# Moving the last cell's value products eleven steps later, and the first output pair's sums and halves thirteen, in a conditional attention kernel

## The chip, the cores and the metric

The kernel runs on one core of one Trainium2 chip. The metric is the device time of one execution in microseconds, shown as the median of several runs.

## The reference

The input x is 32 sequences of 128 rows by 1024 columns in fp32. Two residual layers are applied:

```python
w = weights[conditions]                       # one 128x128 matrix for each sequence
x = x + einsum('bct,bcd->bdt', x, w)          # first layer
q, k, v = proj(x, Wq) * min(cond, 4), proj(x, Wk), proj(x, Wv)    # 16 heads of 64
scores = einsum('bhqd,bhkd->bhqk', q, k) / 8, causal mask, softmax
out = einsum('bhqk,bhkd->bhqd', attn, v)
x = x + einsum('bsd,ed->bse', out, Wo)        # second layer
```

All products are done in fp32 accuracy: each operand is split into a high and a low half (names ending in H and L), and a product is three matmuls (high by high, low by high, high by low; lines 710 to 712).

## The kernel before

The 32 sequences are taken in eight groups of four. Attention goes by **cells**: a cell is one group and two heads for each of q and k; there are 64 cells, n = 0 to 63, of 16 **steps** each. A step is three 128x512 matmuls on TensorE. Every other operation of every engine has a time in steps in a table (an `At`), and each engine's program walks the same times in order and issues what stands there. So the tables fix the order on each engine, and semaphores fix the rest; an instruction that waits holds everything behind it on its engine. The order is also that of the DMAs: SP and ACT both issue DMAs, and a DMA that stands behind a wait on its engine is issued only after it.

The part of the program that matters starts at `T_END`, the end of the last cell's projections. I write **step 20** for `T_END` + 20. The names used are these:

- **Scores and softmax of cell 63** at steps 5 to 12; the transposed probabilities are moved by ten small DMAs (line 1530, at step 15), split by ACT (`half_at`, line 1045, step 25) and POOL (`ptl_at`, line 1336, steps 25.75 and 27.25) into `t_PS`, and multiplied with the values by TensorE (`pv_at`, line 815). A cell has two such **value products**, P = 126 and 127 for the last one, into one PSUM tile `p_PV`. After each, ACT copies (`other_at`, lines 1052 and 1053), DVE sums (`own_at`, line 1229) and POOL adds (`at_at`, line 1339) the result, and SP stores it (line 1656). The second product waits for the DVE sums of the first (`dve_M`).
- **Plain output steps**: steps 0 to 63, eight blocks o = 0 to 7 of eight steps, each block into one of the three banks `p_PJ`. DVE adds a block to the rows of x that SP loaded (line 1266; call it **sum o**), and SP stores it (line 1680, **store o**). SP loads the rows for o = 4 to 7 (line 1511, **row load o**) into the tile of o - 4, after store o - 4 has landed.
- **Output pairs**: from `T_PAIR` = step 64 on, 14 pairs q of 28 steps. A pair needs only seven products of four steps each (i = 0 to 6, line 710 to 712 into `p_LP` and `p_SC`, or `p_PJ` for odd q) in place of eight. POOL forms four sums of the attention rows (`S_add`, lines 1359 to 1369), ACT and DVE split seven operands into halves (`A_high`, line 1080, and `A_low`, line 1239; **half 0 to 6**). The products take halves in the order 0, 4, 1, 5, 3, 2, 6. ACT copies product 0 (line 1088, `f_at`), DVE gathers the others (`c_at`, lines 1250 to 1261), POOL adds x (line 1377).
- **Loads around them**: SP loads the attention rows of pairs 0 and 1 (line 1586, `yp_load`, steps 24 and 24.25) and x of pairs 0 and 1 (line 1598, `xp_load`). ACT issues the last three quarter pairs of Wo from its own queue (line 965, `O_fetch`): 2 x 1 MB each at steps 26.5 (k = 6), 38.5 (k = 4) and 46 (k = 7). I call them **fetches 6, 4 and 7**. They have only a wait for TensorE's last projection, long past.

The waits that matter later are few: product 2 waits for ACT's copy of product 0, which for q = 0 waits until the store of P = 126 has landed, since they share a tile; product 3 waits for the first gather, for q = 0 also for the store of P = 127; POOL's first sum of pair 1 waits for half 6 of pair 0; x of pair 0 is loaded when store 7 has landed; product 6 waits for the fourth gather, which needs POOL's three additions of x.

```python
v = a + (27.25 + 3.25 * k if last else 29 + 4.5 * k)   # a is step 5 for the last cell
early = t - PAIR                                        # t is step 64 for q = 0
```

Of the kernel before, what the change touches and what calls it, by code (L numbers as in the profile page):

```python
# [17 lines left out]
PAIR = 28  # L18
# [27 lines left out]
def cond_attention(nc, x, idx, cond, w0, wq, wk, wv, wo, mask_d, ident_d, out):  # L46
# [14 lines left out]
    with ExitStack() as ctx:  # L61
# [182 lines left out]
        def block(kind, item):  # L244
            bank_of[kind, item] = len(order) % 3
            before[kind, item] = order[-3] if len(order) >= 3 else None
            order.append((kind, item))
# [62 lines left out]
        for p in range(2, NP):  # L310
            t = T_SEV + PAIR * (p - 2)
# [5 lines left out]
        for c in range(4):  # L317
            T_load.put((10, 13, 30, 39)[c], c)
            for i in range(4):
                t = (24, 33, 42, 51)[c] + i  # L320
# [3 lines left out]
        for p in range(2, NP):  # L324
            t = T_SEV + PAIR * (p - 2)
# [25 lines left out]
        for m in range(16):  # L351
            t = T_SEV + PAIR * (2 + m // 2) + (10.5, 23.25)[m % 2]
# [9 lines left out]
        for j in range(NGRP):  # L362
            t0 = T_ATT + STEPS * j
            for c in range(NC):
                n = 4 * j + c
                for i, kind in enumerate("qk"):
                    block(kind, n)
                    for d in range(DC):
                        step_at.put(t0 + 16 * c + 8 * i + d, (kind, n, d))
                done = t0 + 16 * c + 8  # L370
                late = 2.5 if n else 0
                q_ev.put(done + late, n)
                ql_ev.put(done + late + 1, n)
                done += 8
                kh_ev.put(done + 0.25, n)
                kl_ev.put(done + 1, n)
                a = done + 5
                for u in range(GB):
                    k = u // 2
                    sc_at.put(a + k, GB * n + u)  # L380
                    mask_at.put(a + 1 + 2 * k, GB * n + u)
                    exp_at.put(a + (2, 3, 4, 5)[u], GB * n + u)
                move_at.put(a + 10, n)
                for k in range(2):
                    P = 2 * n + k
                    recip_at.put(a + 4 + 2 * k, P)
                    norm_at.put(a + 4.25 + 2 * k, P)
                    turn_at.put(a + 7.5 + 1.5 * k, P)
                    last = n == 4 * NGRP - 1
                    half_at.put(a + (20 if last else 25.25) + 0.5 * k, P)  # L390
                    ptl_at.put(a + (20.75 if last else 26) + 1.5 * k, P)
                    v = a + (27.25 + 3.25 * k if last else 29 + 4.5 * k)
                    own = v + (1.75 if n >= 4 * NGRP - 2 else (1.75, 8.5)[k])
                    for z in range(2):
                        pv_at.put(v, 2 * P + z)
                    other_at.put(v + 0.75, P)
                    own_at.put(own, P)
                    at_at.put(own + 1.25, P)

            if j and j != NG:  # L400
                for i in range(8):
                    X_load.put(t0 - STEPS + ((25.5, 41.5)[i // 4] if j in (1, NG + 1) else (9.5, 25.5, 41.5)[i // 3]), (j, i))
            for k in range(2):
                V_load.put(t0 + ((-11, 2.75)[k] if j == 0 else -38.5 + 16 * k if j == NG else -6.5), (j, k))
            for u in range(GB):
                v_split.put(t0 + ((17, 19, 27.75, 28.75)[u] if j == 0 else 3.75 + u + 14 * (u // 2)), (j, u))
        t = T_ATT + STEPS * (NG - 1)
# [7 lines left out]
        for b in range(GB):  # L415
            t = T_END + (-70.5, -54.5, -38.5, -22.5)[b]
# [30 lines left out]
        yp_load, xp_load, S_add, A_high, A_low, R_at, f_at, c_at, x_at, o_store = (At() for _ in range(10))  # L447
        for q in range(NPAIR):
            t = T_PAIR + PAIR * q
            early = t - PAIR  # L450
            yp_load.put(T_END + (24, 24.25)[q] if q < 2 else t - PAIR - 8, q)
            xp_load.put(t + 5 if q == 0 else t - PAIR + 8, q)
            for i in range(4):
                S_add.put(early + (1, 3, 7, 12)[i], (q, i))
            for i in range(7):
                A_high.put(early + (1, 2, 3, 5.5, 6.5, 10, 15)[i], (q, i))
                A_low.put(early + (2, 3, 4, 6.5, 7.5, 11, 16.5)[i], (q, i))
                R_at.put(t + 4 * i, (q, i))
            f_at.put(t + 4.25, q)
            for i, d in enumerate((8, 12, 16, 20, 24, 28)):  # L460
                c_at.put(t + d + 0.25, (q, i))
                if i in (1, 3, 4, 5):
                    o_store.put(t + d + 1, (q, i))
            for i, d in enumerate((11, 13, 17.5) if q == 0 else (5, 10, 17.5)):
                x_at.put(t + d, (q, i))
# [1255 lines left out]
```

## Time and profile before

| what | before |
|---|---|
| median of 3 runs | 1570.99 us (1570.8 to 1571.9) |
| span of the profiled execution | 1569.4 us |
| runs less span | 1.6 us, taken as the execution's time around its span |
| TensorE busy | 1559.1 us (99%) |
| DMA traffic | 341 MB, mean 218 GB/s |

The profile is of one execution; times in it are from the start of its span. TensorE is busy nearly all the time, so the kernel's time is TensorE's work at its clock plus the few times in which it waits. "q1" is the DMA queue of SP, "q10" that of ACT; both use the same 16 DMA engines.

### The profile page before, as it was taken

Reading aid. Unit: us, or ns where it says so; the run is one execution under the profiler, and the core shown is the slowest. Engines: PE = TensorE matmul, PEld = TensorE weight load, DVE = VectorE, ACT = ScalarE, POOL = GpSimd, SP = SyncE. Lnnn points to the kernel's source line nnn. Section 1 sums busy time; section 2 is a strip of 40 time slices with the busy share of each in tenths; the row PEclk is TensorE's granted clock in tenths of the full one; section 3 lists DMA queues with packets and bytes.
Section 4 is the critical chain, followed back from the end, with each engine's and each line's share of the span. In section 5 each row is a group of like instructions: output and inputs, shape, how many; then the busy total and the mean of one; then the engine's idle time right before and its main releaser. Section 6 shows DMA issues by size and latency. Waiting matters only on the chain.

```text
span 1569.4 us, 23424 instructions
## 1 busy us (share of the span) xinstructions
PE 1559.1 (99%) x7563; PEld 1311.9 (84%) x7563; DVE 980.4 (62%) x1748; ACT 818.9 (52%) x2221; POOL 856.6 (55%) x752
## 2 busy tenths in 40 slices
PE   9999999999999999999999999999999999999999
PEld 7888888888888888888888888888888878888887
DVE  6844454443367777777766777777777754555553
ACT  6645545543366666666666666666666522222220
POOL 1545645643255566557555566675577544555552
PEclk9999999999999999999999999999999999999999
DMA  9958888865856766667677466666675696444442
GB/s 329 334 212 275 307 285 297 301 214 215 308 182 197 206 207 199 210 188 199 186 240 238 152 172 212 186 182 201 182 195 159 222 367 238 168 161 167 163 163 85
DMA packets 192299, 341.46 MB, mean 218 GB/s; under 512 B 23986, under 2 KB 116402, under 8 KB 185010
## 3 DMA queue, kind: packets, MB, share of 16 engines
q1 hardware_dynamic: 191026, 331.59, 65.8%
q10 hardware_dynamic: 1152, 8.39, 1.4%
q8 instruction: 60, 0.98, 0.3%
q14 instruction: 61, 0.50, 0.1%
HBM read 184.70 MB, written 134.22 MB: 203 GB/s over the span
## 4 chain that ended last, share of the span: by engine, by line
PE 98%; DMA 1%; SPq 1%; POOL 0%; issue 0%; DVE 0%; ACT 0%; DVEq 0%
PE p_PJ L710 22%; PE p_PJ L711 22%; PE p_PJ L712 22%; PE p_SC L712 6%; PE p_SC L711 6%; PE p_SC L710 6%; PE p_PV L815 4%; PE p_LP L710 1%; PE p_PV L710 1%; PE p_PV L712 1%; PE p_PV L711 1%; PE p_LP L711 1%; PE p_LP L712 1%; PE p_PV L841 1%; PE p_LP L841 1%; DMA out<-t_xr 1%
## 5 line engine op out<-in xcount | busy, mean ns | idle before, releaser
L711 PE MATMUL p_PJ<-t_XL,t_WH 128*128 128x512 f32 x1008 | 394.1, 391 | 0.0
L710 PE MATMUL p_PJ<-t_XH,t_WH 128*128 128x512 f32 x1008 | 394.1, 391 | 0.0
L712 PE MATMUL p_PJ<-t_XH,t_WL 128*128 128x512 f32 x1008 | 392.1, 389 | 0.0
L1035 ACT ACTIVATE t_PP<-t_PP,t_st 128x128 f32<-128x128 f32 x512 | 199.5, 391 | 175.4 <-DVE t_st L1211 173.9
L1333 POOL TENSOR_TENSOR t_PP<-t_PP,t_st 128x512 f32<-128x512 f32 x128 | 133.4, 1042 | 205.7 <-DVE t_st L1215 205.7
L712 PEld LDWEIGHTS p_PJ<-t_XH,t_WL 128*128 128x128 f32 x1008 | 189.3, 188 | 40.4
L710 PEld LDWEIGHTS p_PJ<-t_XH,t_WH 128*128 128x128 f32 x1008 | 190.0, 188 | 33.8
L711 PEld LDWEIGHTS p_PJ<-t_XL,t_WH 128*128 128x128 f32 x1008 | 190.0, 188 | 32.3
L1229 DVE TENSOR_REDUCE t_AT<-p_PV 64x256 f32<-64x512 f32 x252 | 171.2, 679 | 23.7 <-ACT t_AC L1053 12.0
L1339 POOL TENSOR_TENSOR t_AT<-t_AT,t_AC 128x256 f32<-128x256 f32 x126 | 117.2, 930 | 125.5 <-DVE t_AT L1229 125.5
L1336 POOL TENSOR_TENSOR t_PS<-t_PT,t_PS 128x512 fp32r<-128x512 f32 x122 | 157.7, 1293 | 0.0
L1205 DVE SCALAR_TENSOR_TENSOR t_PP<-p_SC,t_beta,t_mask 128x256 f32<-128x256 f32 x256 | 111.6, 478 | 44.4 <-PE p_SC L712 44.4
L1322 POOL TENSOR_TENSOR t_xl<-t_XT,t_xh 128x512 fp32r<-128x512 f32 x56 | 74.0, 1322 | 94.9 <-ACT t_xh L917 94.2
L1215 DVE RECIPROCAL t_st<-t_st 128x4 f32<-128x4 f32 x128 | 22.9, 179 | 142.0 <-ACT t_PP L1035 142.0
L1022 ACT ACTIVATE t_KH<-p_PJ 64x512 fp32r<-64x512 f32 x128 | 76.1, 595 | 47.8 <-PE p_PJ L712 46.2
L1052 ACT ACTIVATE t_AC<-p_PV 64x256 f32<-64x256 f32 x128 | 48.9, 382 | 95.9 <-PE p_PV L815 94.4
L1035 ACT ACTIVATION_READ_ACCUMULATOR t_PP<-t_PP,t_st 128x1 f32 x512 | 95.6, 187 | 0.0
L1327 POOL TENSOR_TENSOR t_VV<-t_VX,t_VV 128x512 fp32r<-128x512 f32 x64 | 81.4, 1293 | 25.2 <-ACT t_VV L999 25.2
L1192 DVE TENSOR_TENSOR t_KL<-p_PJ,t_KH 64x512 fp32r<-64x512 f32 x128 | 88.2, 689 | 11.0 <-ACT t_KH L1022 7.0
L1211 DVE TENSOR_REDUCE t_st<-t_PP 128x2 f32<-128x256 f32 x256 | 94.2, 409 | 0.0
L815 PE MATMUL p_PV<-t_PS,t_VV 128*128 128x256 f32 x512 | 82.8, 285 | 3.7 <-POOL t_PS L1336 3.7
L815 PEld LDWEIGHTS p_PV<-t_PS,t_VV 128*128 128x128 f32 x512 | 75.2, 192 | 9.3 <-POOL t_PS L1336 4.1
(254 smaller groups left out, 3545.8 us busy)
## 6 DMA issues: line engine op xcount, KB each, us to landing
t_XH<-xth_scratch SPq DMA_DIRECT2D x56, 512.0 KB, 6.5
t_XL<-xtl_scratch SPq DMA_DIRECT2D x56, 512.0 KB, 6.9
t_PT<-t_TB SPq DMA_DIRECT2D x580, 32.0 KB, 2.3
v_scratch<-t_VR SPq DMA_DIRECT2D x64, 256.0 KB, 4.5
xth_scratch<-t_XH SPq DMA_DIRECT2D x16, 1024.0 KB, 4.0
xtl_scratch<-t_XL SPq DMA_DIRECT2D x16, 1024.0 KB, 6.5
t_VX<-v_scratch SPq DMA_DIRECT2D x32, 512.0 KB, 5.7
at_scratch<-t_AT SPq DMA_DIRECT2D x126, 128.0 KB, 3.5
```

The costliest lines, as they stand in the source:

```text
L710: pe.matmul(bank, lh, rh, start=first, stop=False, skip_group_check=goes_on)
L711: pe.matmul(bank, lh, rl, start=False, stop=False, skip_group_check=goes_on)
L712: return pe.matmul(bank, ll, rh, start=False, stop=last, skip_group_check=goes_on)
L815: mm = pe.matmul(PV2[:, z, 256 * h:256 * h + 256], VV[j % 2][:, u, 2 * c + h, :], moving, start=True, stop=True)
L1035: act.activation(PP[:, u, h, :], PP[:, u, h, :], ACT.Exp, bias=st[:, 0, u, h:h + 1], scale=1.0, accum_out=st[:, 1, u, h:h + 1]).then_inc(a ...
L1192: dve.tensor_tensor(KL[r, :, k], pj[r], KH[r, :, k].bitcast(f32), ALU.subtract).then_inc(dve_k, 1)
L1205: dve.scalar_tensor_tensor(out=PP[:, u], in0=SC[u // 2][:, 256 * (u % 2):256 * (u % 2) + 256].rearrange("p (h k) -> p h k", h=2), scalar=b ...
L1211: dve.tensor_reduce(st[:, 0, u, :], PP[:, u], AX, ALU.max, negate=True).then_inc(dve_m, 1)
L1229: dve.tensor_reduce(at_tile(P)[r], both, AX, ALU.add).then_inc(dve_M, 1)
L1333: pool.tensor_tensor(pp, pp, r, ALU.mult).then_inc(pool_n, 1)
L1336: pool.tensor_tensor(p_half(P, 1), p_raw(P), p_half(P, 0).bitcast(f32), ALU.subtract).then_inc(pool_pt, 1)
L1339: pool.tensor_tensor(at_tile(P), at_tile(P), AC[:, P % 2], ALU.add).then_inc(pool_at, 1)
```

## The change

Two numbers of the table change. The value products of cell 63 go from steps 32.25 and 35.5 to steps 43.25 and 46.5, and with them the copies, sums, additions and stores behind them, which are placed relative to `v`. For pair 0 `early` goes from step 36 to step 49, and with it the four POOL sums and the seven halves on ACT and DVE. No load's place in the table is changed, on SP or ACT, and nothing is added or removed.

```diff
-                    v = a + (27.25 + 3.25 * k if last else 29 + 4.5 * k)
+                    v = a + (38.25 + 3.25 * k if last else 29 + 4.5 * k)
...
-            early = t - PAIR
+            early = t - PAIR + (13 if q == 0 else 0)
```

**ACT**, from fetch 6 on (`t_WH`, `t_WL` first), with the copies behind the value products (lines 1052, 1053) and halves 0 and 1 of pair 0 (line 1080); the second `t_WH`, `t_WL` is fetch 4:

```order
 L965 DMA t_WH<-woh_scratch 128x2048
 L965 DMA t_WL<-wol_scratch 128x2048
-L1052 ACTIVATE t_AC<-p_PV 64x256
-L1053 ACTIVATE t_AC<-p_PV 64x256
-L1052 ACTIVATE t_AC<-p_PV 64x256
-L1053 ACTIVATE t_AC<-p_PV 64x256
-L1080 ACTIVATE t_VH<-t_PP 128x512
-L1080 ACTIVATE t_VH<-t_PT 128x512
 L965 DMA t_WH<-woh_scratch 128x2048
 L965 DMA t_WL<-wol_scratch 128x2048
```

Fetch 4 stood behind both copies and two halves; now it stands directly behind fetch 6. Fetch 7 (`t_XH`, `t_XL`) stood behind half 3 and now stands between the two copies.

**SP**, from row load 6 and store 3 on, to the loads of x of pair 0 (the stores with `at_scratch` are those of P = 126 and 127):

```order
 L1511 DMA t_LATE<-x_scratch 128x512 [waits store_out2]
 L1680 DMA out<-t_LATE 128x512 [waits out_row]
+L1511 DMA t_LATE<-x_scratch 128x512 [waits store_out3]
+L1680 DMA out<-t_xr 128x512 [waits out_row]
 L1656 DMA at_scratch<-t_LATE 128x256 [waits at_out]
-L1511 DMA t_LATE<-x_scratch 128x512 [waits store_out3]
+L1680 DMA out<-t_xr 128x512 [waits out_row]
 L1656 DMA at_scratch<-t_LATE 128x256 [waits at_out]
-L1680 DMA out<-t_xr 128x512 [waits out_row] x2
 L1680 DMA out<-t_LATE 128x512 [waits out_row] x2
 L1598 DMA t_xr<-x_scratch 128x1024 [waits store_out2,store_out3,store_out1,store_out0]
```

The store of P = 126 now stands behind row load 7, which waits until store 3 has landed; both stores of the last cell stand later among the output stores.

**DVE**, from half 3 of pair 0 on (`t_PTL` are halves 4 and 5, `t_QL` is half 6, the sums of line 1266 with `t_LATE` are sums 6 and 7, `t_XL` are halves of pair 1):

```order
 L1239 TENSOR_TENSOR t_VL<-t_WR,t_VH 128x512 [waits pair_high]
+L1266 TENSOR_TENSOR t_LATE<-p_PJ,t_LATE 128x512 [waits load_x1_2,o_block]
 L1239 TENSOR_TENSOR t_PTL<-t_WR,t_PTH 128x512 [waits pair_high]
 L1239 TENSOR_TENSOR t_PTL<-t_PP,t_PTH 128x512 [waits pair_high]
-L1266 TENSOR_TENSOR t_xr<-p_PJ,t_xr 128x512 [waits load_x1_1,o_block]
+L1266 TENSOR_TENSOR t_LATE<-p_PJ,t_LATE 128x512 [waits load_x1_3,o_block]
 L1239 TENSOR_TENSOR t_QL<-t_AC,t_QH 128x512 [waits pair_high]
-L1266 TENSOR_TENSOR t_LATE<-p_PJ,t_LATE 128x512 [waits load_x1_2,o_block]
-L1266 TENSOR_TENSOR t_LATE<-p_PJ,t_LATE 128x512 [waits load_x1_3,o_block]
 L1239 TENSOR_TENSOR t_XL<-t_Y,t_XH 128x512 [waits pair_high] x3
```

Half 4 now stands behind sum 6 with its row load, and half 6 behind sum 7; both stood ahead of these sums.

## Rows read from the trace of the kernel before

**Rows 1.** The page, busy time of an engine and the chain by engine.

```profile
PE 1559.1 (99%) x7563; PEld 1311.9 (84%) x7563; DVE 980.4 (62%) x1748; ACT 818.9 (52%) x2221; POOL 856.6 (55%) x752
...
PE 98%; DMA 1%; SPq 1%; POOL 0%; issue 0%; DVE 0%; ACT 0%; DVEq 0%
```

**Rows 2.** Waits of TensorE, whole span: us in total, times, longest.

```profile
PE p_PV L815 <- POOL t_PS L1336: 3.7, 1, 3.7
PE p_LP L710 <- POOL t_wl L1317: 1.7, 1, 1.7
```

**Rows 3.** Timeline of TensorE: start, duration, line, operation, idle before.

```profile
1260.60 0.64 PE L815 MATMUL p_PV<-t_PS,t_VV 128*128 128x256 f32 x4
...
1270.45 0.39 PE L710 MATMUL p_PJ<-t_WH,t_XH 128*128 128x512 f32 x1
...
1274.96 1.23 PE L815 MATMUL p_PV<-t_PS,t_VV 128*128 128x256 f32 x4 [3.67 <-POOL t_PS L1336]
...
1299.78 0.39 PE L710 MATMUL p_LP<-t_WH,t_VH 128*128 128x512 f32 x1
...
1316.10 0.39 PE L710 MATMUL p_SC<-t_WEH,t_QH 128*128 128x512 f32 x1
```

**Rows 4.** Windows: engines' busy time, then PEclk, DMA share, GB/s.

```profile
5.00:10.00 5.00, 3.31 (x15) 2.38 (x14) 3.45 (x5) 3.38 (x7) 1.36 (x2) 1.00 0.90 303
...
1272.00:1300.00 28.00, 25.04 (x102) 20.84 (x103) 14.26 (x18) 5.82 (x12) 15.25 (x12) 0.88 1.01 381
1275.00:1281.00 6.00, 6.00 (x19) 5.08 (x20) 1.38 (x2) 0.85 (x3) 1.87 (x2) 0.52 0.99 363
1288.00:1296.00 8.00, 8.00 (x37) 6.64 (x36) 6.94 (x8) 1.90 (x3) 5.35 (x5) 1.00 1.02 422
```

**Rows 5.** Chain that ended last, before and in the wait: start, duration, what.

```profile
1247.44 0.47 PE p_PV L815 x4
...
1254.03 7.90 DMA out<-t_xr
...
1269.32 2.07 DMA at_scratch<-t_AT
```

**Rows 6.** Timeline of POOL, the low halves for both value products of cell 63.

```profile
1273.65 2.49 POOL L1336 TENSOR_TENSOR t_PS<-t_xr,t_PS 128x512 fp32r<-128x512 f32 x2
```

**Rows 7.** Timeline of ACT: issues of fetches 6, 4, 7, and half 0.

```profile
1271.52 0.44 ACTq L965 DMA_DIRECT2D t_WL<-wol_scratch  x1
...
1284.31 0.63 ACT L1080 ACTIVATE t_VH<-t_PP 128x512 fp32r<-128x512 f32 x1 [2.62 <-DMA t_PT<-at_scratch]
1284.40 0.33 ACTq L965 DMA_DIRECT2D t_WH<-woh_scratch  x1
...
1288.54 0.33 ACTq L965 DMA_DIRECT2D t_XH<-woh_scratch  x1
```

**Rows 8.** DMA queues, window 1276 to 1278: packets, MB, share of 16 engines.

```profile
q10 hardware_dynamic: 85, 0.59, 86.4%
q1 hardware_dynamic: 84, 0.10, 13.4%
```

**Rows 9.** Timeline of SP's DMA issues.

```profile
1276.17 0.38 SPq L1586 DMA_DIRECT2D t_PP<-at_scratch  x1
...
1281.90 0.43 SPq L1680 DMA_DIRECT2D out<-t_LATE  x1
...
1289.62 0.32 SPq L1511 DMA_DIRECT2D t_LATE<-x_scratch  x1
...
1303.39 0.80 SPq L1598 DMA_DIRECT2D t_xr<-x_scratch  x2
```

**Rows 10.** Landing of row load 7, then store 7: count, size, us to landing.

```profile
t_LATE<-x_scratch SPq DMA_DIRECT2D x1, 256.0 KB, 7.5
...
out<-t_LATE SPq DMA_DIRECT2D x1, 256.0 KB, 2.6
```

**Rows 11.** Timelines of DVE and POOL behind value product and sum 7.

```profile
1262.09 1.41 DVE L1229 TENSOR_REDUCE t_AT<-p_PV 64x256 f32<-64x512 f32 x2 [1.20 <-ACT t_AC L1053]
...
1299.98 0.69 DVE L1266 TENSOR_TENSOR t_LATE<-p_PJ,t_LATE 128x512 f32<-128x512 f32 x1 [4.75 <-PE p_PJ L712]
...
1307.97 1.30 POOL L1377 TENSOR_TENSOR t_xr<-t_xr,t_LATE 128x512 f32<-128x512 f32 x1 [9.54 <-DMA t_xr<-x_scratch]
...
1313.58 0.69 DVE L1261 TENSOR_TENSOR t_xr<-p_SC,t_xr 128x512 f32<-128x512 f32 x1 [1.26 <-PE p_SC L712]
```

## The prediction

> **What bounds the kernel now.** The page comes first: TensorE is busy 99% of the span and the chain that ended last is 98% TensorE [rows 1]. So an edit counts only if it changes TensorE's work, its waits or its clock. The waits of TensorE come second: there are four in all, and one is late in the program, 3.7 us before the first value product of cell 63, ended by POOL's low half [rows 2]. The timeline shows its place: step 32 is issued at 1270.45, the value product only at 1274.96 [rows 3]. The windows show a second cost: from 1275 to 1281 the granted clock is 0.52, that is mostly the lower level of 1.2 GHz, where it is 1.00 before [rows 4]. The chain shows why the low half was late: store 0 took 7.90 us to land, SP stood behind it and then issued ten small moves and a store that landed 2.07 us after 1269.32; a DVE sum needed that store, and POOL stood behind the sum [rows 5]. POOL's two low halves then ran from 1273.65 to 1276.14 [rows 6]. The change leaves all of that where it is and lets TensorE do eleven output steps first.
>
> **Term 1, the wait that goes.** A step is 0.68 us: products 0 to 5 of pair 0 are 24 steps from 1299.78 to 1316.10 [rows 3]. A value product at full clock takes 0.47 us [rows 5]. Without a wait and at full clock the rest up to pair 0 would be 1270.45 + 0.68 = 1271.13, plus 31 steps (21.1) and two value products (0.9), so 1293.2 instead of 1299.78: **6.6 us** earlier. Of these 3.7 are the wait and 2.9 the low clock. In the new order the first value product is due at 1271.13 + 11 x 0.68 = 1278.6, and the low halves are done at 1276.14: covered by 2.5 us for both, 3.7 for the first alone. The banks of the blocks before it are free, since sums 2 and 3 are far behind TensorE's demand.
>
> **Term 2, a small new wait.** The second value product stands three steps behind the first, 0.47 + 2.04 = 2.5 us at full clock. It needs DVE's sums of the first; in the cell before these ended at 1262.09 + 1.41 = 1263.50, that is 2.9 us after a product at 1260.60 [rows 3, 11]. So it waits 0.4 us. At half clock this was hidden. Pair 0 could start at **1293.6**, its product 6 at 1293.6 + 16.3 = **1309.9**, against 1316.10.
>
> **Term 3, what the moved work held back.** This decides. In ACT's program fetch 4 stood behind two copies and half 0, which waited for the attention rows until 1284.31; so it went out at 1284.40 and fetch 7 at 1288.54 [rows 7]. Now nothing that waits stands between fetch 6 and fetch 4: it goes out right behind 1271.52, and fetch 7 behind the first copy, near 1279.4. ACT's queue then holds 6 MB without the pause from 1280 to 1286 in which SP's queue moved the attention rows. While both queues have work they take turns packet by packet, 85 against 84 in two microseconds, but ACT's packets are 8 KB and SP's 1 to 2 KB, so SP gets 13% of the time [rows 8]. The Trainium skill (DMA: Bandwidth & Descriptors, Queues, rings and completion order) also has each engine take turns by packets; by that rule, the trace agrees, large packets win.
>
> SP's queue is served in order, so I ask when store 3 lands, since row load 7 waits for it. Ahead of it and with it are, issued since 1271: 2 row loads, 1 store and 2 stores of attention rows, 2 MB for pairs 0 and 1, and store 3 itself, 3.4 MB; ACT's three fetches are 6.3 MB. The engines are full from 1272 to 1300 at 381 GB/s [rows 4]; 9.7 MB take 25.4 us, so store 3 lands near **1297.4**, where it was 1289.6, when row load 7 was issued [rows 9]. From there the chain is read off before's own:
> - row load 7 issued 0.1 later, landing 2.6 us after, like store 7 on quiet engines [rows 10]: 1300.1. Sum 7 follows.
> - from the start of sum 7 to POOL's first addition of x is 1307.97 - 1299.98 = 8.0 us (store 7 lands 2.6 after its issue, x is then loaded at 1303.39) [rows 9, 11], so 1308.1.
> - from there to the end of the fourth gather 1313.58 + 0.69 - 1307.97 = 6.3 us [rows 11], so product 6 starts at **1314.4**.
>
> The other new order on DVE gives nearly the same: half 6 stands behind sum 7, POOL's sums for pair 1 behind half 6, and the first gather behind two halves of pair 1. I count 0.7 + 0.7 + 1.3 + 1.3 + 0.7 + 0.7 + 0.7 = 6.1 us (seven operations of the lengths in [rows 11]) from sum 7 to product 3, 1306.2, and three products of 2.72 later product 6, 1314.4. Earlier waits are absorbed in this: half 0 must wait for attention rows landing near 1294, so product 0 starts about 2 us late; half 4 stands behind sum 6 and costs product 1 about as much.
>
> **Sum.** Product 6 at 1314.4 instead of 1316.10 is 1.7 us less. Behind it nothing is moved, so the rest shifts as it is. The span becomes 1567.7 and the time, with the same 1.6 us around it, **1569.3 us** against the median of 1570.99: -0.1%. Bounds of term 3: at the 422 GB/s of a stretch with mostly ACT's packets [rows 4] store 3 lands at 1295.0 and the time is 1566.9; at 363 GB/s [rows 4] it lands 1.3 later, and if row load 7 takes 1 us more, 1571.6. The main case's own range is 1566.9 to 1571.6. About 0.2%, 3.1 us, is what a measurement can tell from no change.
>
> **Rivals.**
> 1. *The loads hold.* If ACT's fetches do not push SP's loads back and DVE's order costs nothing, all but 0.4 of the 6.6 us is won: 1564.8. For it: total DMA traffic is unchanged and the engines had work all the time before as well. Against: x of pair 0 can't come before store 7, and even before, 14.3 us passed from sum 7 to the end of the fourth gather. 12%.
> 2. *Equal shares by bytes.* If the queues shared time evenly, SP's 3.4 MB would be through at half of 381 GB/s in 17.8 us, near 1289.8, as before; row load 7 would then take its 7.5 us under load [rows 10], sum 7 start at 1297.4 and product 6 at 1311.7: 1566.6. For it: at 1289.62 row load 7 could go out in spite of fetch 4. Against: [rows 8]. 14%.
> 3. *The clock falls again.* Three waits of 1 to 2 us stand close together ahead of products 0, 1 and 3. One of 1.7 us early in the program left the clock at 1.00, one of 3.67 us brought it to half [rows 2, 3, 4]; it decides from somewhere between. If it falls in front of product 3, the stretch at 1.2 GHz costs 2.9 us as in term 1: 1572.2. A fall ahead of products 0 or 1 is absorbed. The Trainium skill (TensorE: Matmul & The Clock Gate, A second HAM failure mode: psum-queue depth-cycling) says that frequent short idles between groups of matmuls can make the clock go back and forth; by that rule this case is the forecast, and the early waits here do not show it. 15%.
> 4. *Slower: row load 7 lands late.* Place: SP's queue at 1297.5, where stores 4 and 5, two stores of attention rows and row load 7 are released together. If it takes the 7.5 us of before instead of 2.6 [rows 10], product 6 starts at 1319.3 and the time is 1574.2. It ends above no change by 3.1 us from a landing of 7.4 us on. Against: those 7.5 us were under ACT's fetches, which are through by then. 13%.
>
> That the change doesn't do what it says can be left out: the order lists show the moves.
>
> **How the numbers follow.** The main case has 46%, of which 8% lie below 1567.9 and 38% within 0.2%. Faster by over 0.2%: 8 + 12 + 14 = 34%. Slower: 13, and 2 of the clock's 15, so 15%. Within: 38 + 13 = 51%. The range reaches from 1565.0, just short of rival 1, to 1574.3, rival 4 at its price, and leaves out about 2 in 10.
>
> **What would show it.** Right: no wait before the first value product, no half clock at 1275, some 0.4 us before the second; fetch 4 issued near 1272; the loads for pair 0 landing near 1294 instead of 1284; waits before products 0 to 3; row load 7 issued near 1297; product 6 near 1314. Wrong: a wait of no product in pair 0 and product 0 near 1293.6 (rival 1), row load 7 out near 1290 (rival 2), a half clock between 1294 and 1312 (rival 3), or row load 7 landing after 1304 (rival 4).

## The result, and the profile after

| what | before | after |
|---|---|---|
| median of 5 runs each, same chip | 1571.36 us (1570.80 to 1572.25) | 1576.71 us (1575.99 to 1579.14) |
| span of the profiled execution | 1569.4 us | 1574.7 us |

The ratio is 1.0038 (95% interval 1.0027 to 1.0049): by this ratio the change makes the kernel **slower by 0.38%**; the medians are 5.3 us apart. I had put no change first, at 1569.3 us, and the result lies outside my range.

(One slip ahead of the prediction: fetch 7 stood behind half 4 before the change, not half 3. Nothing was worked out from it.)

The page of the profile after shows TensorE busy 1.4 us longer than before [rows 1], with the same number of instructions, and less of the chain on it: 95% in place of 98%.

```profile
PE 1560.5 (99%) x7563; PEld 1312.2 (83%) x7563; DVE 983.3 (62%) x1748; ACT 818.0 (52%) x2221; POOL 857.2 (54%) x752
...
PE 95%; DMA 2%; POOL 1%; DVE 1%; SPq 1%; issue 0%; ACT 0%; DVEq 0%; ACTq 0%
```

TensorE's waits, to hold against [rows 2] (total, times, longest):

```profile
PE p_LP L710 <- DVE t_VL L1239: 3.3, 1, 3.3
PE p_LP L710 <- POOL t_wl L1317: 2.3, 1, 2.3
PE p_SC L710 <- DVE t_PTL L1239: 1.8, 1, 1.8
PE p_SC L710 <- DVE t_XL L1239: 1.4, 1, 1.4
...
PE p_PV L815 <- DVE t_LATE L1229: 0.3, 1, 0.3
```

The 3.7 us before the first value product are gone. In their place stand 0.3 before the second, 3.3 before product 0, 1.8 before product 1 and 1.4 before product 3, together 6.8. TensorE's timeline gives the places, against [rows 3]:

```profile
1271.16 0.39 PE L710 MATMUL p_PJ<-t_WH,t_XH 128*128 128x512 f32 x1
...
1279.32 0.64 PE L815 MATMUL p_PV<-t_PS,t_VV 128*128 128x256 f32 x4
...
1282.36 0.71 PE L815 MATMUL p_PV<-t_PS,t_VV 128*128 128x256 f32 x4 [0.34 <-DVE t_LATE L1229]
...
1297.95 0.72 PE L710 MATMUL p_LP<-t_WH,t_VH 128*128 128x512 f32 x1 [3.29 <-DVE t_VL L1239]
...
1304.33 0.50 PE L710 MATMUL p_SC<-t_WH,t_PTH 128*128 128x512 f32 x1 [1.77 <-DVE t_PTL L1239]
...
1313.07 0.47 PE L710 MATMUL p_SC<-t_XH,t_PTH 128*128 128x512 f32 x1 [1.40 <-DVE t_XL L1239]
...
1321.31 0.39 PE L710 MATMUL p_SC<-t_WEH,t_QH 128*128 128x512 f32 x1
```

From step 32 to product 6 it is 50.15 us, and was 1316.10 - 1270.45 = 45.65: **4.5 us more**. (Step 32 itself comes 0.7 later in this execution; most of that is the wait of 2.3 for `t_wl` at the start of the program in place of 1.7.) Of the 4.5 us, 6.8 - 3.7 = 3.1 are waits; the other 1.4 are the clock and the restarts behind waits. The windows show the half clock gone at 1275 and back twice, behind the waits before products 0 and 1:

```profile
1275.00:1281.00 6.00, 6.00 (x30) 5.02 (x29) 0.88 (x2) 0.76 (x2) 2.35 (x2) 1.00 0.99 383
1298.00:1301.50 3.50, 3.50 (x9) 2.73 (x10) 3.50 (x3) 1.49 (x3) 3.42 (x3) 0.51 0.18 67
1304.00:1308.00 4.00, 3.67 (x10) 2.91 (x11) 4.00 (x6) 1.38 (x4) 1.70 (x2) 0.61 0.55 208
```

**Why product 0 was late.** ACT's timeline, against [rows 7]: fetch 4 goes out right behind fetch 6, fetch 7 behind the first copy, and half 0 waits for the attention rows until 1296.04 instead of 1284.31.

```profile
1272.69 0.44 ACTq L965 DMA_DIRECT2D t_WL<-wol_scratch  x1
...
1273.17 0.44 ACTq L965 DMA_DIRECT2D t_WH<-woh_scratch  x1
...
1280.00 0.33 ACTq L965 DMA_DIRECT2D t_XH<-woh_scratch  x1
...
1296.04 0.63 ACT L1080 ACTIVATE t_VH<-t_PP 128x512 fp32r<-128x512 f32 x1 [12.14 <-DMA t_PT<-at_scratch]
```

SP's timeline, against [rows 9], has the other side:

```profile
1278.43 12.74 SPq L1586 DMA_DIRECT2D t_Y<-at_scratch  x2
...
1292.92 0.66 SPq L1680 DMA_DIRECT2D out<-t_LATE  x1
...
1300.49 0.32 SPq L1511 DMA_DIRECT2D t_LATE<-x_scratch  x1
```

The two issues for pair 1's rows take 12.74 us; they were 1.84 before. Store 3 is issued only at 1292.92, and row load 7, which waits for its landing, at 1300.49; before, the last was at 1289.62. What the DMA engines did in the meantime is in the queues' part for 1278 to 1290 (packets, MB, share of 16 engines), the same view as [rows 8]:

```profile
q10 hardware_dynamic: 580, 4.24, 85.2%
q1 hardware_dynamic: 579, 0.69, 15.8%
```

For 12 us the queues took turns packet for packet, and SP moved 0.69 MB while ACT moved 4.24. Before the change SP's queue had most of the same 12 us (window 1278 to 1290 of before):

```profile
q1 hardware_dynamic: 2921, 3.22, 78.3%
```

**Why products 1 and 3 were late.** DVE's timeline; the sum at 1304.80 is sum 7, which answers to the one at 1299.98 in [rows 11], and the last row is the first gather:

```profile
1296.70 1.20 DVE L1239 TENSOR_TENSOR t_VL<-t_PP,t_VH 128x512 fp32r<-128x512 f32 x1 [10.88 <-ACT t_VH L1080]
1297.82 3.44 DVE L1239 TENSOR_TENSOR t_VL<-t_PT,t_VH 128x512 fp32r<-128x512 f32 x2
...
1303.60 0.68 DVE L1239 TENSOR_TENSOR t_PTL<-t_WR,t_PTH 128x512 fp32r<-128x512 f32 x1
...
1304.80 0.69 DVE L1266 TENSOR_TENSOR t_LATE<-p_PJ,t_LATE 128x512 f32<-128x512 f32 x1
...
1305.99 4.07 DVE L1239 TENSOR_TENSOR t_XL<-t_Y,t_XH 128x512 fp32r<-128x512 f32 x3
...
1312.29 0.68 DVE L1250 TENSOR_TENSOR t_LATE<-p_SC,t_LATE 128x512 f32<-128x512 f32 x1
```

DVE is busy without a pause from 1296.70 to the end of the gather at 1312.97, and product 3 starts 0.1 us behind it (the waits above put this down to line 1239, but its last operation had ended at 1312.36). A low half takes 1.2 to 1.8 us up to 1302.95, then 0.68. POOL's timeline has the reason: from 1297.43 to 1302.41 and again from 1306.22 it runs its own sums, and these are longer too, 1.6 to 1.7 us each where POOL alone takes 1.3.

```profile
1300.68 1.73 POOL L1369 TENSOR_TENSOR t_AC<-t_PT,t_WR 128x512 f32<-128x512 f32 x1
1306.22 1.59 POOL L1359 TENSOR_TENSOR t_WR<-t_Y 128x512 f32<-128x512 f32 x1 [3.82 <-DVE t_QL L1239]
```

The trace of before, which I read too narrowly, had both lengths: beside POOL and with POOL idle.

```profile
1290.67 1.77 DVE L1239 TENSOR_TENSOR t_PTL<-t_WR,t_PTH 128x512 fp32r<-128x512 f32 x1
...
1300.70 1.90 DVE L1239 TENSOR_TENSOR t_XL<-t_Y,t_XH 128x512 fp32r<-128x512 f32 x3
```

### The profile page after: what moved, and what is told of

Read it like the earlier page. It is cut to its first block, busy times and chain, and to the rows that moved or that the text cites. A ratio compares the mean times of both kernels' runs of the same rounds, so it can differ in the third digit from the quotient of the medians.

```text
span 1574.7 us, 23424 instructions
## 1 busy us (share of the span) xinstructions
PE 1560.5 (99%) x7563; PEld 1312.2 (83%) x7563; DVE 983.3 (62%) x1748; ACT 818.0 (52%) x2221; POOL 857.2 (54%) x752
## 4 chain that ended last, share of the span: by engine, by line
PE 95%; DMA 2%; POOL 1%; DVE 1%; SPq 1%; issue 0%; ACT 0%; DVEq 0%; ACTq 0%
PE p_PJ L710 22%; PE p_PJ L711 22%; PE p_PJ L712 21%; PE p_SC L712 6%; PE p_SC L710 6%; PE p_SC L711 6%; PE p_PV L815 4%; PE p_PV L710 1%; PE p_PV L712 1%; PE p_PV L711 1%; DMA t_PT<-at_scratch 1%; PE p_LP L710 1%; PE p_LP L712 1%; PE p_LP L711 1%; PE p_PV L841 1%; PE p_LP L841 1%
```

## The experiments

Theories. **L** (loads): fetches 4 and 7, released early, starve SP's queue. **O** (order): the halves' new place on DVE costs time by itself. **S** (store): with the fetches back, the store of P = 126, now behind row load 7, holds ACT's copy of product 0 and with it product 2. Each run was timed in five rounds next to the kernel before on the same chip (medians before: 1571.81 us for e1 to e4, 1571.39 for f1 to f4, 1571.5 for g1 to g4). All steps below are table numbers.

**e1: the fetches back at their old place in ACT's order.** After, with

```diff
-  (6, 26.5, 26.5), (4, 38.5, 38.5), (7, 46, 46)
+  (6, 26.5, 26.5), (4, 51.5, 51.5), (7, 59, 59)
```

> The whole change, with fetches 4 and 7 also thirteen steps later, so that ACT's order is that of the kernel before. Theory L (the loads: ACT's fetches ahead of time starve SP's queue): the attention rows of pair 0 land within 1 us of before, near 1285, half 0 is ready before product 0, the long waits before products 0 and 1 go, and the time is 1564 to 1568, 4 to 7 us below the kernel before. Theory O (the order: halves and sums of pair 0 too late on DVE, behind sums 6 and 7): fetches don't matter and it stays within 1.5 us of the change, 1575 to 1578. Theory S (SP's order: stores of the last cell behind row load 7): product 2 waits 2 us and more, 1567 to 1570.

Measured: 1571.5 us, ratio 1.0000 (0.9991 to 1.0009). The 5.3 us are gone and products 0, 1 and 3 wait for nothing, but nothing is gained either, and the time lies above what both L and S said. TensorE's timeline, then ACT's:

```profile
1303.94 0.77 PE L710 MATMUL p_LP<-t_WH,t_VH 128*128 128x512 f32 x1 [3.64 <-ACT t_LATE L1088]
```

```profile
1286.09 0.63 ACT L1080 ACTIVATE t_VH<-t_PP 128x512 fp32r<-128x512 f32 x1 [1.99 <-DMA t_PT<-at_scratch]
...
1303.20 0.60 ACT L1088 ACTIVATE t_LATE<-p_LP 128x512 f32<-128x512 f32 x1 [6.56 <-DMA at_scratch<-t_LATE]
```

The attention rows are on time, but product 2 waits for the copy that needs the store of P = 126: issued at 1293.26, landed 9.8 us later. The clock falls behind that wait (0.50 from 1303.9 to 1308). So S has the place but not the size, and the wait removed at 1275 has moved to 1304.

**e2: the early fetches alone.** Before, with fetches 4 and 7 at 27 and 34, where the change in effect puts them.

```diff
-  (4, 38.5, 38.5), (7, 46, 46)
+  (4, 27, 27), (7, 34, 34)
```

> The kernel before, with only ACT's fetches 4 and 7 at steps 27 and 34, which gives exactly the ACT order of the change; value products, sums and halves where they were. Theory L: SP's issues for pair 1 stall as in the change (over 10 us for two instead of 1.8), attention rows of pair 0 land 10 us or more later than 1284, near 1295, TensorE waits in pair 0, and the time rises by 2 to 5 us over before, 1573 to 1576.5. The wait of 3.7 us before the value product stays. Theory O and theory S: no difference from before, within 1 us.

Measured: 1578.19 us, ratio 1.0040 (1.0026 to 1.0054), the loss of the change with neither of its moves, and 1.7 us above the range that L gave. SP's issue is held as long (SP's timeline); TensorE waits before block 7, whose bank is freed by a sum behind the late halves on DVE:

```profile
1278.66 12.65 SPq L1586 DMA_DIRECT2D t_Y<-at_scratch  x2
```

```profile
1299.94 0.79 PE L710 MATMUL p_PJ<-t_WH,t_XH 128*128 128x512 f32 x1 [5.14 <-DVE t_xr L1266]
```

**e3: eleven in place of thirteen for the halves.**

```diff
-  early = t - PAIR + (13 if q == 0 else 0)
+  early = t - PAIR + (11 if q == 0 else 0)
```

> The whole change, with the halves and sums of pair 0 eleven steps later instead of thirteen. On DVE half 4 is then ahead of sum 6 and half 6 ahead of sum 7, as before; ACT's and SP's order are those of the change. Theory L: the attention rows still land near 1296, so the time stays within 1.5 us of the change (at most one DVE operation of 0.7 us less in front of product 1, and POOL's sums for pair 1 some 0.7 us earlier), 1575 to 1577. Theory O: most of the loss goes, 1567 to 1572.

Measured: 1578.34 us, ratio 1.0036 (1.0022 to 1.0049), 1.3 us above L's range and far from O's. No difference from the change can be seen. In the profiled execution the rows of pair 0 landed at 1298.5, later still than in after, and the waits before products 0, 1 and 3 were 5.7, 0.8 and 3.4 us: while the rows are this late, the place of half 6 can't be told from their scatter. f2 puts the question again without it.

**e4: the halves alone.** Before, with `early` thirteen later and the value products left.

```diff
-  early = t - PAIR
+  early = t - PAIR + (13 if q == 0 else 0)
```

> The kernel before, with only the sums and halves of pair 0 thirteen steps later, value products not moved. Fetches 4 and 7 then stand behind both copies and ahead of all halves, so both go out near 1282 instead of 1284.4 and 1288.5. The wait of 3.7 us and the half clock stay. Theory L: most attention rows for pair 0 have landed or started by then, they land at 1284 to 1288; time within 2 us of before, 1570 to 1573.5. Theory O: the late halves cost what the change lost and did not win, 1576 and more.

Measured: 1576.92 us, ratio 1.0035 (1.0022 to 1.0049). O's number came out and L's did not, but not by O's way alone. Fetches 4 and 7 went out at 1281.68 and 1282.53, behind the second copy. The rows of pair 0 were in time (half 0 at 1285.24), row load 6 was not, and in the new order halves 4 and 6 stand behind sums 6 and 7. DVE's timeline:

```profile
1300.07 0.69 DVE L1266 TENSOR_TENSOR t_LATE<-p_PJ,t_LATE 128x512 f32<-128x512 f32 x1 [7.12 <-DMA t_LATE<-x_scratch]
```

So the halves' move alone releases the fetches, and a small load of SP that is in flight then pays; the new order on DVE hands that on, and product 3 waited 3.08. The value products' move was not run alone. By the table fetch 4 would then still stand behind halves 0 and 1.

**f1: fetches back, and the store of P = 126 ahead of row load 7.** e1 with row load 7 a quarter of a step behind that store:

```diff
-  x1_load.put(T_END + ((-4, -4, 8, 10)[o] if o < 4 else 8 * o - 20), o)
+  x1_load.put(T_END + ((-4, -4, 8, 10)[o] if o < 4 else 46.5 if o == 7 else 8 * o - 20), o)
```

> The change with fetches 4 and 7 thirteen steps later (as in the first run) and row load 7 at step 46.5 instead of 36, so that the store of P = 126 is issued ahead of it, as before the change. In the first run product 2 waited 3.6 us for that store. Theory C (a chain of blockers, each hiding the next: stores, then DVE's halves behind sum 7, which waits for row load 7): the wait of product 2 goes, and product 3 waits 3 to 5 us for DVE's first gather instead; the start of product 6 gains at most 1.5 us and the time is 1569.5 to 1573. Theory S alone (the store was all that was left): no wait over 1 us in pair 0, 1565 to 1567.

Measured: 1574.84 us, ratio 1.0022 (1.0013 to 1.0032), above what I expected. Product 2's wait is gone and product 3 has a longer one: it was hidden behind it. TensorE, then DVE:

```profile
1309.95 0.76 PE L710 MATMUL p_SC<-t_XH,t_PTH 128*128 128x512 f32 x1 [7.43 <-DVE t_XL L1239]
```

```profile
1301.75 0.69 DVE L1266 TENSOR_TENSOR t_LATE<-p_PJ,t_LATE 128x512 f32<-128x512 f32 x1 [7.57 <-DMA t_LATE<-x_scratch]
...
1302.96 4.02 DVE L1239 TENSOR_TENSOR t_XL<-t_Y,t_XH 128x512 fp32r<-128x512 f32 x3
```

Row load 7 was issued at 1292.63 and landed 9 us later, under fetches 4 and 7; behind it come half 6, then POOL's sums and pair 1's halves side by side, 4.02 us for three.

**f2: f1 with eleven in place of thirteen** (fetches 4 and 7 at 49.5 and 57, to keep their place in ACT's order). Half 6 then stands ahead of sum 7.

> The same, with sums and halves of pair 0 (and fetches 4 and 7 with them) eleven steps later instead of thirteen, so that half 6 is ahead of sum 7 on DVE and POOL forms the sums of pair 1 early. Theory C: product 3 waits 1 to 2.5 us instead of 3 to 5, product 6 is then limited by x of pair 0 (14.3 us behind sum 7, which starts near 1299.5); 1568 to 1570.5. A theory that DVE's order doesn't matter: equal to the run with thirteen within 0.7 us.

Measured: 1571.18 us, ratio 1.0002 (0.9993 to 1.0011), 3.7 us under f1 but above the 1568 to 1570.5 that I expected; product 3 still waited 3.1. DVE's timeline:

```profile
1301.29 0.69 DVE L1266 TENSOR_TENSOR t_LATE<-p_PJ,t_LATE 128x512 f32<-128x512 f32 x1 [6.78 <-DMA t_LATE<-x_scratch]
1301.90 1.89 DVE L1239 TENSOR_TENSOR t_XL<-t_Y,t_XH 128x512 fp32r<-128x512 f32 x3
```

Sum 7 is as late as in f1, but POOL's sums of pair 1 are done by then, and the three halves take 1.89. So O is real: the order with thirteen costs 3.7 us where row load 7 is late. What is left is that row load.

**f3: f2 with pair 1's attention rows at step 33**, to take 1 MB from in front of row load 7, and **f4**, the same edit on the kernel before.

```diff
-  yp_load.put(T_END + (24, 24.25)[q] if q < 2 else t - PAIR - 8, q)
+  yp_load.put(T_END + (24, 33)[q] if q < 2 else t - PAIR - 8, q)
```

> The same again, with SP's load of the attention rows of pair 1 at step 33 instead of 24.25, behind row load 6 and store 3. Theory C: store 3 lands 4 to 5 us earlier, near 1288, row load 7 near 1295, sum 7 starts by 1296, nothing waits over 1 us in pair 0 and the whole 6 us are there: 1564.5 to 1567. If the engines' backlog as such is the limit (all bytes are the same), no gain over the run before, 1568 to 1570.5.

> The kernel before with only that load of pair 1 at step 33. Its bound is the wait of 3.7 us before the value product and the low clock behind it, which this doesn't touch: every theory expects the time of before within 1 us, 1570.5 to 1572.5.

Measured: f3 1571.14 us, ratio 1.0000 (0.9991 to 1.0009); f4 1571.68 us, ratio 1.0000 (0.9991 to 1.0009). f3 missed its number. Row load 7 was issued 4.4 us earlier, at 1287.76, and landed no sooner (DMA view of f3, 1288 to 1302, last number from issue to landing):

```profile
t_LATE<-x_scratch SPq DMA_DIRECT2D x1, 256.0 KB, 14.3
```

So moving this load of SP did not help while ACT's 4 MB were in the engines.

**g1 and g2: the fetches' bytes.** The change and the kernel before, with fetches 4 and 7 issued where they are but 256 columns wide in place of 2048 (a column slice on both sides of line 965's DMA). Both kernels leave out the other 1792 columns, 3.7 MB of Wo, so their results are not the kernel's; they serve for the time alone.

> The change as it is, with every place in every queue kept, but fetches 4 and 7 load only 256 of 2048 columns (the rest of these quarters of Wo is left out, so 3.7 MB less). Theory B (the bytes of these fetches, moved ahead of SP's loads, are the whole loss): SP's issues for pair 1 take about 2 us again instead of 12.7, row load 7 goes out before 1289, no wait over 1 us in pair 0, half clock gone, and the 6.2 us are won: 1564 to 1567. If the new order on SP and DVE costs something by itself, 1568 and more.

> The kernel before with the same 3.7 MB left out. Its wait of 3.7 us before the value product lies ahead of these fetches, so theory B expects no change: within 1 us of before, 1570.5 to 1572.5. It is the measure for the run with the change.

Measured: g1 1567.09 us, ratio 0.9971 (0.9960 to 0.9983); g2 1571.18 us, ratio 0.9998 (0.9989 to 1.0007). The largest wait of g1 from the value products on (its lines are one further on):

```profile
PE p_SC L710 <- DVE t_XL L1240: 1.1, 1, 1.1
```

This run decides for L. Without the bytes the same change is worth -4.4 us, with them +5.3; before the change they cost nothing, 1571.18 against 1571.5. SP's two issues took 2.46 us in g1 and half 0 ran at 1286.33. Three numbers missed, the last two by 0.1: row load 7 left at 1292.81, where I had it before 1289, the wait is 1.1 where I had at most 1, and the time is just above my 1567. The slice also makes each packet an eighth as long, so g1 doesn't tell the bytes from the length of the packets.

**g3: the fetches moved one place earlier each, with the change.** Fetch 5 goes to 0.5, 6 to fetch 5's old place at 8, 4 to 26.5 and 7 to 49.5, so two fetches instead of three fall between 1272 and 1300; row load 7 at 46.5 and eleven steps as in f2. **g4**: the same fetches on the kernel before, with fetch 7 at 38.5 and nothing else.

```diff
-  (5, 8, 8), (2, 9.5, 9.5), (6, 26.5, 26.5), (4, 38.5, 38.5), (7, 46, 46)
+  (5, 0.5, 0.5), (2, 9.5, 9.5), (6, 8, 8), (4, 26.5, 26.5), (7, 49.5, 49.5)
```

> A whole kernel that tries to keep the gain: the change, with sums and halves eleven steps later, row load 7 at step 46.5, and ACT's fetches moved one place up: fetch 5 at step 0.5 (where the engines have room), fetch 6 at step 8, fetch 4 at 26.5, fetch 7 at 49.5. Theory B: as 2 MB are gone from the full stretch, row load 7 lands before 1295 and at most 1 us of waiting is left in pair 0; 1565 to 1568. If the moves of cell 63 behind store 0 come later by the new fetch, the slack of 3.7 us takes up to that. If the limit is not these bytes, 1570 and more.

> The kernel before with only the fetches one place up (fetch 5 at step 0.5, 6 at 8, 4 at 26.5, 7 at 38.5). Theory B: the wait before the value product is set by store 0 and the ten moves, which are ahead; it may change by 1 us either way, and so the time: 1570 to 1573. It tells how much of a gain of the run before is due to the change's two moves.

Measured: g3 **1568.14 us, ratio 0.9984 (0.9975 to 0.9993)**; g4 1573.15 us, ratio 1.0010 (1.0001 to 1.0019). g3 is the best full kernel here, 3.4 us under before and some 8.5 under the change, at 0.1 above my range; row load 7 landed at 1298.6 (1294.94 + 3.7), where I had it before 1295. Its largest wait of TensorE there, and one window over pair 0's first products, with the clock whole:

```profile
PE p_SC L710 <- DVE t_XL L1239: 1.4, 1, 1.4
```

```profile
1296.00:1312.00 16.00, 14.62 (x65) 11.84 (x64) 9.27 (x14) 3.52 (x6) 9.80 (x7) 1.00 0.76 274
```

g4 shows that the earlier fetches don't pay by themselves: the wait before its value product was 5.9 us. They need the eleven steps of slack which the change gives.

## Why the prediction was wrong

**Term 1, right.** No wait and no half clock at 1275; the value product is issued straight behind its step. g1 banks most of it: 4.4 of the 6.2 us left after term 2; 1.1 us of the difference is its wait before product 3.

**Term 2, right.** 0.34 us against 0.4.

**Term 3, right about what is held back, wrong about which part of it decides, and undersized.** That product 6 would come at 1314.4 is the number that failed; it came at 1321.31, and 1569.3 + 6.9 = 1576.2 us is the time that these runs gave. Product 3, which I had at 1306.2, came at 1313.07, and 8.2 us as forecast followed. (Some 0.7 us of the clock times are this execution's later start.) Laid along my own path the 6.9 us stand in three places:

1. *Store 3 landed 3.0 us late*, 1300.4 for 1297.4, and row load 7 took 3.0 us in place of 2.6: **3.4 us**. I divided 9.7 MB by the 381 GB/s of before. As many MB passed from 1272 to 1300 after, but not evenly: 73 GB/s in the first 2 us (252 in before), since fetch 6 left 1.2 us later, then 389 up to 1298.5, and hardly anything until store 3 was in. In between the engines moved 413 GB/s while ACT's large packets lasted and 349 once only SP's small ones were left. Windows of after, the rate last in each row:

```profile
1272.00:1274.00 2.00, 2.00 (x11) 1.65 (x10) 1.35 (x2) 1.15 (x2) 0.00 (x0) 1.00 0.43 73
...
1278.00:1290.00 12.00, 11.66 (x56) 9.50 (x55) 3.35 (x5) 1.51 (x4) 1.47 (x2) 1.00 1.02 413
1293.00:1297.00 4.00, 1.66 (x8) 1.05 (x6) 0.30 (x1) 0.96 (x2) 0.92 (x1) 1.00 1.10 349
...
1298.50:1300.40 1.90, 1.90 (x6) 1.51 (x5) 1.90 (x2) 0.63 (x1) 1.82 (x2) 0.50 0.09 32
```

2. *Sum 7 waited for DVE*, **1.3 us**: it ran at 1304.80, its row load had landed at 1303.5, and halves of pair 0 at 1.2 to 1.8 us each stood ahead of it. I had priced only what stands behind sum 7.
3. *From sum 7 to product 3 it was 8.3 us, not 6.1*: **2.2 us**. I took each operation at its length alone [rows 11]; beside POOL three of pair 1's halves took 4.07 us instead of 1.90. f1 against f2 tests this step: with the late row load, the order with thirteen costs 3.7 us.

**The step that failed is the path: "Earlier waits are absorbed in this".** DVE waits for nothing from 1296.70 to product 3, so the landing of row load 7 at 1303.5 held nothing. The work behind the late attention rows did. The chain that ended last says the same; it comes from these rows and passes POOL's sums, ACT and DVE (after, window 1284 to 1322):

```profile
1277.79 18.22 DMA t_PT<-at_scratch
...
1306.08 4.19 DVE t_XL L1239 x4
```

Behind the rows stood 15 operations of DVE, from half 0 to the gather, and they took 1312.97 - 1296.70 = 16.3 us. I had the rows at 1294, they were in at 1296.0, and I had priced seven of the fifteen, at the lengths that they have beside an idle POOL. With row load 7 on time and the rows as late as here, sum 7 would still have been at 1304.80. That is read from the trace; no run has this case by itself. In f1, where the rows were in time, it was row load 7 that decided.

The other chain that I worked out, by store 7 and the load of x, was sized well: 1312.28 - 1304.80 = 7.5 us from sum 7 to POOL's first addition, where I had 8.0. It did not decide; it would have put product 6 at 1312.28 + 6.3 = 1318.6.

**Product 0.** Attention rows near 1294 were in fact at 1296.0; the wait was 3.3 us instead of 2, and the clock fell behind it and again behind the next. That a fall ahead of products 0 and 1 would be absorbed held: product 3 still waited 1.4 us.

**The rivals.** Rival 1 (loads hold) gave 1564.8, and g1, where they nearly hold, 1567.1. Rival 2 (equal shares) is out: 580 packets to 579 over 12 us, and 85.2% of the time to 15.8%. Rival 3's falls came, but in the places where they are absorbed. Rival 4 had the right sign and, at 1574.2, came nearest, but not by its path: it has row load 7 issued at 1297.5 and landing 7.5 us later, at 1305.0. The load was issued at 1300.49 and landed in 3.0 us, at 1303.5, and sum 7 waited for DVE and not for it.

**The chances.** What failed besides is the range. Both chains were priced with the lengths of a quiet DVE and quiet DMA engines, so they could only fail together and upwards; the range treated them as free to go both ways.

**Left open.** g1 gains 4.4 us and not 6.2. In its profile step 32 to product 6 takes 1312.34 - 1271.26 = 41.08 us, 4.6 less than before; of the 6.6 us of term 1, waits of 0.3 and 1.1 take a part, and some 0.6 were not traced. Also open is what exactly holds SP's issue for 12.7 us. No variant was run that splits the fetches into small packets. The wait before the first value product in the old order was 3.7, 4.2, 4.3, 5.9 and 6.8 us in profiles of before, g2, e2 and e4, g4 and f4, so a gain read from one profile is uncertain by as much.

## What to carry to other kernels

When an instruction that waits is moved on an engine that also issues DMAs, list the DMAs that stood behind it: the wait was their throttle, and here 4 MB that had been held back by chance starved the small loads and stores of the other queue. Price elementwise chains at the length that the operation has beside its neighbour engine's work, which the trace of before shows if the rows are picked by time and not by shape. Where an engine has no idle time between a late load and the product that waits, a second late load on its path decides nothing: follow the chain from the first. And take a bottleneck's removal as an opening for the next one in line (1275, then 1304, then 1310 here): ask for each what waits directly behind it before counting the gain.

## What the runs showed of the hardware that I had not expected

- **An issue can stall with the queue.** Two DMA issues on SP took 12.74 us in after and 12.65 in e2 while ACT's fetches filled the engines, 12.70 in e3, and 1.62 to 2.46 in e1, e4, f1, f2, g1 and g3. The second of the two alone took 9.97 us in after, with no wait of the program between them. So the DMAs behind are not only late to land but late to be issued. The Trainium skill (DMA: Bandwidth & Descriptors, Rules for kernel authors) says of spreading DMAs over several issuing engines that it doesn't help bandwidth and "only saves sequencer issue time"; no run here tests the first part, since every kernel issues from both SP and ACT. But the share of the two queues was 4.24 MB to 0.69, and SP lost issue time by it.
- **DVE and POOL slow each other.** A low half on DVE took 0.68 us with POOL idle and 1.7 to 1.8 beside POOL's sums, and those 1.6 to 1.74 instead of 1.3. The two run in step, one of each in 1.7 us. The Trainium skill (SBUF — State Buffer, Who interferes with whom) has a `tensor_tensor` with both inputs in SBUF contend with GpSimd's reads, over a pair of ports that it calls an exclusive lock. The alternation agrees with it, while sums that read PSUM (line 1266) kept their 0.69.
- **Which waits brought the clock down.** Waits of 3.3 (after), 3.64 (e1), 3.08 (e4) and 3.1 us (f2), and the longer ones of e2, e3 and f1, were each followed by a stretch at 1.2 GHz (granted clock 0.50 to 0.6 in the windows behind them), and so was the 1.8 us of after, which ended 2.9 us behind the slow stretch before it (1301.46 to 1304.33). The 1.2, 2.3 and 1.1 us of f3, the 1.1 of g1 and the 1.4 of g3 left it at 2.4 GHz (1.00).
